# 16-head attention: how the split keys travel to their stacked tile, and when the next context is sent for

## The reference

```python
q = split(layernorm(x) @ Wq.T + bq)          # 16 heads of 8 numbers
k = split(ctx_1024 @ Wk.T + bk)
v = split(ctx_1024 @ Wv.T + bv)
scores = einsum('bhqd,bhkd->bhqk', q, k) / sqrt(8)
scores = where(mask == 0, -1e9, scores)      # L1 only
out = einsum('bhqk,bhkd->bhqd', softmax(scores), v)
x = x + merge(out) @ Wo.T + bo
```

## Time and profile before

| what | us |
|---|---|
| time, median of 3 runs (lowest, highest) | 5002.61 (5001.39, 5007.9) |
| the profiled execution: its own time | 4999.51 |
| the profiled execution: its span, first to last instruction | 4997.5 |
| TensorE busy | 4035.6 (81%) |
| VectorE busy | 2670.8 (53%) |
| ScalarE busy | 1974.0 (40%) |
| GpSimd busy | 996.4 (20%) |
| mean granted TensorE clock | 0.898 |

### The profile page before, as it was taken

One profiled execution on the slowest core, in us unless ns is written; L12 is line 12 of the kernel. 1 busy time (PEld: TensorE's weight loads), 2 busy tenths in 40 slices (PEclk: granted clock), 3 DMA queues, 4 the chain that ended last, 5 costly groups with the idle time before them and its releaser, 6 DMA issues. The chain is left out here.

```text
span 4997.5 us, 95999 instructions
## 1 busy us (share of the span) xinstructions
PE 4035.6 (81%) x39918; PEld 2481.6 (50%) x39918; DVE 2670.8 (53%) x3910; ACT 1974.0 (40%) x3760; POOL 996.4 (20%) x979
## 2 busy tenths in 40 slices
PE   7799488887888896788888886357888889888888
PEld 4544266666666543566666664123444444444444
DVE  3233355555554332555555553336777777777751
ACT  3200144444444000344444443204555555555542
POOL 0000211111111002111111111101334333433330
PEclk8799699999998898799999998678999999999988
DMA  8600444455442001443444430001000000000000
GB/s 247 191 0 0 122 122 123 130 130 130 124 121 67 34 0 56 103 100 91 97 100 104 96 92 17 6 5 31 19 19 13 19 19 19 13 19 19 13 1 20
DMA packets 107980, 329.11 MB, mean 66 GB/s; under 512 B 54151, under 2 KB 55247, under 8 KB 107023
## 3 DMA queue, kind: packets, MB, share of 16 engines
q1 hardware_dynamic: 107567, 323.20, 24.7%
HBM read 168.20 MB, written 7.00 MB: 35 GB/s over the span
## 5 line engine op out<-in xcount | busy, mean ns | idle before, releaser
L1701 POOL TENSOR_TENSOR l_S<-l_S,l_shift 125x448 f32<-125x448 f32 (+1 forms) x416 | 459.7, 1136 | 311.3 <-ACT l_shift L1927 306.3
L1165 ACT ACTIVATE L2a_probs<-ps 125x448 f32<-125x448 f32 x768 | 377.3, 543 | 147.4 <-PE ps L1075 133.4
L1165 ACT ACTIVATE L1a_probs<-ps 125x448 f32<-125x448 f32 x768 | 376.9, 542 | 141.2 <-PE ps L1075 127.7
L1755 PE MATMUL ps<-l_wk,l_xnT 128*125 128x512 f32 (+1 forms) x832 | 426.0, 637 | 2.3 <-ACT l_k_squares L1908 1.7
L1773 PE MATMUL ps<-l_G,l_xnT 128*125 128x448 f32 (+1 forms) x832 | 388.7, 549 | 32.6 <-DVE l_S L2024 32.6
L1908 ACT ACTIVATE l_k_squares<-ps 125x512 f32<-125x512 f32 (+1 forms) x416 | 247.7, 596 | 412.6 <-PE ps L1755 412.6
L2004 DVE TENSOR_REDUCE l_norms<-l_k_squares 125x8 f32<-125x512 f32 (+1 forms) x416 | 278.8, 680 | 231.3 <-ACT l_k_squares L1908 229.3
L1198 DVE TENSOR_REDUCE L2a_chunk_max<-ps 112x1 f32<-112x1000 f32 x256 | 298.0, 1195 | 193.7 <-PE ps L1038 193.7
L1198 DVE TENSOR_REDUCE L1a_chunk_max<-ps 112x1 f32<-112x1000 f32 x256 | 297.9, 1195 | 177.0 <-PE ps L1038 177.0
L1805 PE MATMUL ps<-l_S,l_z 125*128 125x448 f32 x768 | 349.6, 545 | 0.0
L1038 PE MATMUL ps<-L2a_keys,L2a_queries 96*112 96x500 f32 x768 | 260.5, 422 | 91.8 <-issue 69.4
(11 more groups left out here) (381 smaller groups left out, 6883.2 us busy)
## 6 DMA issues: line engine op xcount, KB each, us to landing
L1a_keys<-L1a_k_hi SPq DMA_DIRECT2D x256, 187.5 KB
L2a_keys<-L2a_k_hi SPq DMA_DIRECT2D x256, 187.5 KB
a_ctx_T<-in_ctx_T SPq DMA_DIRECT2D x32, 750.0 KB, 11.9
xn<-L_valid SPq DMA_DIRECT2D x32, 750.0 KB, 6.9
L1a_ctx_T<-in_ctx_T SPq DMA_DIRECT2D x32, 750.0 KB, 5.8
L1a_keys<-L1a_k_lo SPq DMA_DIRECT2D x128, 187.5 KB
L2a_ctx_T<-in_ctx_T SPq DMA_DIRECT2D x32, 750.0 KB, 5.8
L2a_keys<-L2a_k_lo SPq DMA_DIRECT2D x128, 187.5 KB
```

The lines of the kernel that those rows point to most:

```text
L1165: nc.scalar.activation(probs[t % NPR][:, h * HQ // 2:(h + 1) * HQ // 2], s.ps[0:KP, i % 3, 0:HQ // 2], ACT.Exp).then_inc(probs_made, 1)
L1701: nc.gpsimd.tensor_tensor(S[b % 2][0:r, t, :], S[b % 2][0:r, t, :], shift[0:r, :], ALU.add)\
L1755: nc.tensor.matmul(s.ps[0:rows(t), t % 2, 0:HID], xnT[b % 2][:, t * KP:t * KP + rows(t)], wk[:, :], start=True, stop=True).then_inc(k_made, 1)
```

## The change

Three things are changed in `attention_16_heads`, for L1 and L2 alike. Keys item 1 of batch b + 2 moves from step 3 into `before_scores`, right behind item 0; the values items move to steps 1 and 3, the sums to step 5. On SP the context of batch b + 3 is sent for ahead of the keys of batch b + 2. And the keys take another way: `k_hi` and `k_lo` are each stored whole (128 partitions, 750 KB) to a DRAM buffer, SP waits for both stores to land, and three loads of 750 KB bring them back, each into 32 partitions of `keys` for all four groups. ScalarE's wait before it overwrites `k_hi` is now for the stores.

```diff
-    PIECES = 12
+    PIECES = 3
-    before_scores = [("rows", 1, 0), ("keys", 2, 0), ("rows", 1, 1)]
+    before_scores = [("rows", 1, 0), ("keys", 2, 0), ("keys", 2, 1), ("rows", 1, 1)]
     step_items = [[("rows", 1, n)] for n in range(2, ROWS)] + [[], []]
-    step_items[2].append(("values", 1, 0))
-    step_items[3].append(("keys", 2, 1))
-    step_items[4].append(("sums", -1, 0))
-    step_items[5].append(("values", 1, 1))
+    step_items[1].append(("values", 1, 0))
+    step_items[3].append(("values", 1, 1))
+    step_items[5].append(("sums", -1, 0))
...
+        parts_dram = nc.dram_tensor(f"{layer}_key_parts", [2, 2, D, SK], F32, kind="Internal").ap()
...
+                sp.wait_ge(k_hi_made, b * 2 + 2)
+                if b >= 2:
+                    sp.wait_ge(keys_moved, (b - 1) * 16 * PIECES)
+                sp.dma_start(parts_dram[b % 2, 0], k_hi[:, :].bitcast(F32)).then_inc(parts_stored, 16)
                 sp.wait_ge(k_lo_made, b * 2 + 2)
-                for g in range(G):
-                    for k, part in enumerate((k_hi, k_lo, k_hi)):
-                        sp.dma_start(keys[b % NKB][k * GR:(k + 1) * GR, g, :].bitcast(F32),
-                                     part[g * GR:(g + 1) * GR, :].bitcast(F32)).then_inc(keys_moved, 16)
+                sp.dma_start(parts_dram[b % 2, 1], k_lo[:, :].bitcast(F32)).then_inc(parts_stored, 16)
+                sp.wait_ge(parts_stored, b * 32 + 32)
+                for k, part in enumerate((0, 1, 0)):
+                    sp.dma_start(keys[b % NKB][k * GR:(k + 1) * GR, :, :].bitcast(F32),
+                                 parts_dram[b % 2, part].rearrange("(g r) c -> r g c", g=G)).then_inc(keys_moved, 16)
...
             for b in range(B):
+                if b + 3 < B:
+                    load_context(b + 3)
                 if b + 2 < B:
                     move_keys(b + 2)
                 if b + 3 < B:
-                    load_context(b + 3)
...
                 if b and n == 0:
-                    act.wait_ge(keys_moved, b * 16 * PIECES)
+                    act.wait_ge(parts_stored, b * 32)
                 nc.scalar.activation(k_hi[:, cols], k_full[:, cols], ACT.Copy).then_inc(k_hi_made, 1)
```

More of the change, by code:

```diff
@@ L894, in attention_16_heads @@
         ctx_loaded, terms_loaded = [[sem(f"{what}_loaded{u}") for u in range(2)] for what in ("ctx", "terms")]
-        valid_loaded, keys_moved = sem("valid_loaded"), sem("keys_moved")
+        valid_loaded, parts_stored, keys_moved = (sem(n) for n in ("valid_loaded", "parts_stored", "keys_moved"))
         neg_moved = [sem(f"neg_moved{n}") for n in range(NKB)]
```

## The result

The changed kernel took 5414.17 us (median; 5407.77 to 5426.02) against 5002.74 for the kernel before: a ratio of 1.082, 95% interval 1.080 to 1.084. It is slower by 411 us, where I had forecast 190, and it lies outside the stated range. The profiled execution's span is 5414.3 us against 4997.5.

What follows compares the result with a forecast made beforehand. It took the chain values item 1, context and stores, loads, next rows as the period: 16.2 + 6.9 + 12.5 + 0.1 = 35.7 us in L2, 36.0 in L1. With +104, +79, +9 and -2 us: 5190, range 4960 to 5310.

Steps and rivals of the forecast that it cites:

- Which chain sets the period: Rows item 0 to the next batch's, through values item 1, context, stores and loads: 35.7 us in L2, 36.0 in L1.
- Context's wait gone: TensorE's 2.18 us wait for the context before the key products goes, as the context is sent for first.
- T0 to values item 1: From a batch's first rows item on TensorE (T0) to values item 1 done: 16.2 us, bounds 15 and 17.5.
- Context and two stores: Three transfers over 128 partitions on SP's queue, scaled from three query stores: 6.9 us, plus 0.3 in L1.
- The signs named in the prediction: Expected in the changed profile, among others: SP waiting about 5 us before the first load, 410 GB/s before the loads.
- Three loads into 32 partitions: Keys back from DRAM, first load's issue to next rows: 12.5 us, at the on-chip key copies' rate.
- The sum: Batch period of 16.2 + 6.9 + 12.5 + 0.1 = 35.7 us in L2, 36.0 in L1.
- The range: Stated 4960 to 5310 us; terms allowed +-1.3, +-0.5 and +1/-1.9 us, not all at once.
- Rival 3: Round trip through DRAM costs 2.5 us more than the query stores show: 5335 us; chance 0.05.
- Rival 1: Loads from DRAM run at full rate, last term 6.9 us, about 4860 us in all; chance 0.14.
- Rival 2: Third load (partitions 64 to 95) flows beside the second, data 7.5 us, about 4975 in all; chance 0.08.
- Rival 4: Context's wait does not hold the stores, values item 1 by T0 + 13: near 5010 us; chance 0.04.

Runs made afterwards that it cites:

- k2: Kernel before with only the context sent for ahead of the keys on SyncE: 5198.04 us, ratio 1.039.
- k9: Changed kernel with the same wait for values item 1, but behind it the two stores first, then the context: 5237.36 us, ratio 1.048.
- k7: Changed kernel with the context sent for between the stores and SyncE's wait for them: 4996.76 us, ratio 0.998.
- k10: Changed kernel with SyncE waiting for the context to land before it sends mask rows and stores: 5418.51 us, ratio 1.084.
- k12: Changed kernel with the keys brought back in twelve loads in place of three, same bytes to same places: 5296.77 us, ratio 1.060.
- k3: Changed kernel with the keys copied on the chip in twelve transfers, no DRAM; new item order and context first kept: 4885.21 us, ratio 0.977.
- k5: Changed kernel with four loads of 96 partitions in place of three of 32, same bytes: 5297.38 us, ratio 1.060.
- k4: Changed kernel with the context sent for behind the keys, which still go through DRAM: 4940.57 us, ratio 0.988.
- k11: k4 with the keys brought back in twelve loads of 187.5 KB in place of three of 750 KB: 4792.51 us, ratio 0.958.

## Why the prediction was wrong

The chain that sets the period was forecast rightly. Two of its three terms were sized too small: context and stores, put at 6.9 us where they took 10.4, and the three loads, put at 12.5 where they took 14. The means used here are those of the table in the result.

- *Which chain sets the period*: right. It runs through the wait for values item 1, context, stores, round trip, loads and next rows. k2, k9 and k7 show it directly: 195 us for the order alone, 241 for taking the stores from behind the wait and 177 for putting the context behind them.
- *Context's wait gone*: right; nothing idles on it in the steady state.
- *T0 to values item 1*, 16.2 us: measured 15.2 in L1 and 15.0 in L2, inside the bounds of 15 and 17.5, and in the other direction than the error of the whole. Rows item 1 starts at T0 + 5.8 in the L1 batch and T0 + 6.7 in the L2 batch, not at T0 + 7.95. In L1 the granted clock was back at 1.00 before the value products, which took 1.37 and not 1.6 us, the next two key products 1.10; rows item 0 and four key products took 4.0 (929.29 to 933.3), not 4.9.
- *Context and two stores*, "For 2.30 MB: 5.5 + 1.35 = 6.9 us": measured 10.3 in L1 and 10.4 in L2. This is the first step that failed. I scaled three stores of one kind down to a load and two stores, as if only bytes counted. A load and two stores sent together gain next to nothing over sending one after the other (k10), and two stores with nothing ahead of them need 5.5 to 6.7 us (k10, k9). The sum of the parts, each with its own landing, would have given 4.1 + 5.5 by k10's batch. The signs named in the prediction missed here too: SyncE waits 8.1 and 8.8 us for the stores (260.0/32 and 281.2/32), not about 5, and the rate before the loads is 180 to 264 GB/s for three microseconds, not 410.
- *Three loads into 32 partitions*, "With three issues in place of twelve I take 12.5 us": measured 14.2 and 13.9. This is the second. The rate was that of the on-chip copies (212 GB/s, 204 to 222 there), as forecast. But I took the time of twelve transfers for three, and even a little less. k12 shows the opposite: twelve are 1.6 us faster, and SyncE needs 6.61 us to issue them, so fewer issues had nothing to give.
- *The sum*: by the means, -1.0 + 3.1 + 1.7 = 3.8 us in L1 and -1.2 + 3.5 + 1.4 = 3.7 in L2. By the turns, a batch is 39.99 - 36.0 = 4.0 and 39.60 - 35.7 = 3.9 us longer than forecast; 29 times each, that is 229 us, and 224 were missing. The first term's error hid over a fifth of the other two.
- *The range*: I combined the errors of the three terms as if they were independent, and capped the stores at +0.5. Even all at once they reach only 5190 + 2.8 x 58 = 5352. A term taken from a different kind of transfer wanted both ends from the rows: the context's own landing of 4.3 to 7.4 us in front of a store pair would have reached 10 us.
- *Rival 3*, the round trip costs 2.5 us more, "reads of the context and writes being mixed": this is close to what happened, at 3.1 and 3.5 us, and I gave it 0.05. Its reason holds in part: the rate is low while load and stores can be in flight together (k9, k10), but keeping them apart gains nothing, for the gap between them costs as much.
- *Rival 1*, full rate from DRAM: fell (192 to 216 GB/s for the most part). The Trainium skill, "SBUF — State Buffer", section "Door 1: The DMA port swizzle", speaks of 189 GB/s for 32 partitions at 1 MiB and 218 at best; the loads' mean of 212 lies between the two, though single windows reach 241.
- *Rival 2*, the third load beside the second: not seen. From 2641 on the rate in the L2 batch is 198, 210, 160 GB/s.
- *Rival 4*, the stores not held by the context's wait: fell. They are issued behind it, at T0 + 15.3 in the L1 batch.

The forecast never priced the parts alone. The item order by itself is worth -374 us, and the other two parts +785 on top of it. I said that the earlier keys buy nothing. For the changed kernel that is not tested: no run has the context first and the way through DRAM with the old item order. With the keys copied on the chip and the context first, the item order as a whole, which also moves the values items, is worth 313 us (k2 to k3). The sign came out right by the chain, with both errors on the same side of it.

## What to carry to other kernels

When a queue issues in order, put what is ready early ahead of what must wait: the same transfers in another order were 417 us faster. Price a load and the stores behind it as a sum of landings, unless a trace shows that such transfers gain by being sent together. A range is only as good as its narrowest term: ask of each whether its nearest row is of the same kind. And try the parts of a change one by one: one part of this one was a 7.5% gain that the other two buried.

## What the runs showed of the hardware

- A load of 750 KB from DRAM with two stores of 750 KB to DRAM behind it took 10.3 to 10.4 us in the mean sent at once (the changed kernel), and 10.1 to 11.4 us with a wait for the load in between (k10). The stores sent first took 6.3 to 6.7 us for both (k9).
- In the first 3 us of the mixed case the engines were busy at 180 to 264 GB/s. The load alone reached 358 and the stores alone 432 GB/s (k10), and in k9 the rate fell from 426 to 228 where the load should have joined the stores. The mechanism is open.
- Twelve loads of 187.5 KB that alternate among three groups of 32 partitions ran at about 238 GB/s, three of 750 KB, one group after the other, at about 212. The Trainium skill, "DMA: Bandwidth & Descriptors", section "Rules for kernel authors", advises to coalesce many small transfers into a large one. With this destination the kernel with fewer and larger loads is the slower one, by 117 us (5414 against 5297); size and alternation are not separated.
- 96 partitions in one load gave 240 to 252 GB/s (k5), a context load over 128 partitions 408.
- TensorE stopped for about 3 us in a batch within a run of value products in k4 and k11, with nothing in the program to wait for. The cause is open.
